# Divisors inverted per pair of token tiles, broadcasts in halves, and rotary sums on VectorE, in an attention block on one core

## Chip, cores and metric

The kernel runs on one core of a Trainium2 chip. The metric is the device time of one execution in microseconds, as the median of several runs.

## What is computed

For four batches of 1024 tokens and 512 channels, the reference does an attention block with a quantised linear layer behind it, each with a residual and a layernorm:

```python
q, k, v = X @ Wq, X @ Wk, X @ Wv               # 16 query heads, 8 key/value heads, 64 wide
q = q * cos + rotate_half(q) * sin             # the same for k
att = 50 * tanh((q @ k.T) / 16 / 50)           # causal mask, then softmax
y = (softmax(att) @ v).reshape(tokens, 1024) @ Wo
x = layernorm(X + y)
q8, scale = int8 of x per token (absmax / 127)
f = float16((q8 @ W8.T) * scale * w_scale + bias)
out = layernorm(x + f)
```

## The kernel before

All matrix products of the attention are done with operands split in a high and a low part of type fp32r (three products for one), written hi and lo in the names. The engines run programs of their own, each in the order written, and meet at semaphores. SyncE (SP) issues the loads and stores from its queue; ScalarE issues some from its own.

**Attention.** A batch is worked through in four units of four query heads and two key/value heads. A unit has 2 x 9 score tiles of 128 keys by up to 1024 query columns (both query heads of a group side by side), numbered s = 0 to 17 in the unit and g = 0 to 71 in the batch. The nine tiles of a key/value head cover four pairs of token tiles, c = 0 to 3 (256 queries each). For each tile TensorE makes the scores (L649), ScalarE takes tanh (L831) and exp (L836), GpSimd sets the causal mask on diagonal tiles (L1241), VectorE rounds to the high part (L1031) and subtracts to get the low part (L1035), and TensorE multiplies with v (L675) three tiles later (LAG). The row sums of the softmax come from a column of ones beside v. When a pair c of a head is finished, ScalarE copies sums and divisors (`keep_sums`, L850) and SP stores them in DRAM (`put_sums`: y_scratch in L447, d_scratch in L450).

**Rotary chunks.** While a unit runs, q and k of the next unit m are projected in three chunks x = 0 (k), 1 and 2 (q), 24 matmuls each, spread over tiles 0 to 2, 5 to 7 and 9 to 11 (L594). VectorE multiplies by cosine and sine (`rope_read`, at s = 3, 8, 12), GpSimd adds or subtracts the two products (`rotate`, L1218, L1221, L1223, at s = 4, 9, 13), ScalarE rounds (`round_rope`, L818, at s = 5, 10, 14), VectorE makes the low part (`rope_low`), and SP copies high and low part into place (`put`, eight DMAs each, L426 and L435). A buffer `work` has two places that alternate between the chunks. The chunks of the second unit of each later batch (m = 5, 9, 13) can't be put during the first unit of the batch in this way; they are projected at the end of the output stage before (`between(m)`), with the puts of x = 0 and 1 there and the rest in tiles 0 to 3.

**Passage.** After the last tile of a batch, TensorE projects v of the next batch (L620, tiles 0 to 4 before the first output tile, 5 to 7 after it; in the last batch there is none). SP loads the divisors of all token tiles (L538), VectorE inverts them (L1045), SP stores them (L546). For each of eight token tiles t, ScalarE's queue loads the reciprocals broadcast over 64 partitions, two DMAs of 256 KB (`load_rb`, L861) into the one buffer rb, SP loads y (L383, three buffers in `work`), GpSimd scales (L1254), ScalarE rounds (L871), VectorE makes the low part (L1049).

**Output stage.** Per token tile t: the product with Wo in two halves (L697), residual and layernorm statistics on VectorE (`residual1`, from L1057), 1/std on GpSimd (L1261, L1263), normalisation on ScalarE, quantisation on VectorE, transposition on TensorE (L707), `keep_q` on ScalarE (L891), the int8 linear layer (`linear`, L717) between the two halves of output tile t + 2, then rescaling, bias, residual and second layernorm. Wo's high and low part (2 MB each) are loaded over the q and k buffers from DRAM (L528, L532); after the first output tile SP loads w_scale, bias and the next unit's weights (w_ring).

The order of ScalarE's program around the stage:

```python
                load_rb(b, 0)
                load_rb(b, 1)
                round_y(b, 0)
                load_rb(b, 2)
                round_y(b, 1)
...
                    if t + 2 < NT:
                        load_rb(b, t + 2)
                    if t + 1 < NT:
                        round_y(b, t + 1)
...
                        keep_q(b, t - 2)
```

## Time and profile before

| | us |
|---|---|
| median of 3 runs (lowest, highest) | 1679.62 (1673.33, 1680.08) |
| profiled execution, its own time | 1678.03 |
| its span, first to last instruction | 1676.3 |
| busy: TensorE, VectorE, ScalarE, GpSimd | 1347.2, 1078.7, 838.9, 522.9 |

A row of the page's groups reads: line, engine and operation, output <- input, shapes, count | busy us in total, mean ns of one | idle time of the engine just before them <- what ended most of it. A row of the timeline reads: start us, duration us, engine, line, operation, output <- input, shapes, count, and in square brackets the idle time before it and its releaser. SPq and ACTq are the DMA queues of SyncE and ScalarE. PEclk is TensorE's granted clock as a share of 2.4 GHz. A row of the windows reads: stretch, its length, busy us (instructions) of PE, PEld, DVE, ACT and POOL, PEclk, busy share of the DMA engines, GB/s.

### The profile page before, as it was taken

To read this page: it belongs to the slowest core of one execution; us is meant where nothing else is said; L and a number is where in the kernel's file an instruction comes from. 1 tells how busy PE (TensorE), PEld (TensorE's weight loads), DVE (VectorE), ACT (ScalarE), POOL (GpSimd) and SP (SyncE) were. 2 spreads that over 40 slices of the span, in tenths; PEclk is the share of its full clock that TensorE was granted. 3 is DMA by queue.
4 is the path that set the end of the run, shared out by engine and by line. 5 is a ranking of instruction groups with operands and counts; after the bars stand their busy time and mean duration, and the time that the engine had idled before them with its cause. 6 is when DMAs were issued, how large, how long until landed. Compare 5 with 4: busy or idle time off the path is not lost.

```text
span 1676.3 us, 17436 instructions
## 1 busy us (share of the span) xinstructions
PE 1347.2 (80%) x5776; PEld 973.7 (58%) x5776; DVE 1078.7 (64%) x1242; ACT 838.9 (50%) x952; POOL 522.9 (31%) x525
## 2 busy tenths in 40 slices
PE   6389997966697999795768999898668799997565
PEld 5366674745464767564546676565445576764343
DVE  3287886843466888782455878776245688886244
ACT  4067666631127776562223867665122486786122
POOL 2351322212453133231245322212134413230244
PEclk9799998997798999898878999999787899999686
DMA  7764444375315244455423333636452514424331
GB/s 279 223 204 127 124 97 138 84 262 139 107 47 145 61 117 102 120 172 181 156 88 104 85 82 104 172 71 204 141 157 63 146 40 114 112 71 170 106 107 44
DMA packets 116138, 212.22 MB, mean 127 GB/s; under 512 B 22608, under 2 KB 65616, under 8 KB 111824
## 3 DMA queue, kind: packets, MB, share of 16 engines
q1 hardware_dynamic: 106320, 185.94, 38.6%
q10 hardware_dynamic: 9728, 25.17, 5.2%
q8 instruction: 46, 0.75, 0.2%
q14 instruction: 44, 0.36, 0.1%
HBM read 105.64 MB, written 38.27 MB: 86 GB/s over the span
## 4 chain that ended last, share of the span: by engine, by line
PE 54%; issue 10%; POOL 9%; DVE 8%; SPq 8%; DMA 5%; ACT 5%; ACTq 1%; POOLq 0%; DVEq 0%
PE ps L675 17%; PE ps L594 11%; PE ps L649 11%; PE ps L697 7%; PE ps L620 5%; SPq L435 4%; POOL y_raw L1254 3%; SPq L426 3%; PE ps L717 2%; ACTq L861 1%; ACT probs L831 1%; DMA x_raw<-X_T 1%; ACT probs L836 1%; POOL work L1223 1%; DMA d_scratch<-sums 1%
## 5 line engine op out<-in xcount | busy, mean ns | idle before, releaser
L675 PE MATMUL ps<-prob_hi,v 128*65 128x512 f32 (+3 forms) x1280 | 419.6, 377 | 31.4 <-DVE prob_lo L1035 31.2
L649 PE MATMUL ps<-qk 128*128 128x512 f32 (+1 forms) x1280 | 328.8, 385 | 80.8 <-ACT probs L831 52.6
L1035 DVE TENSOR_TENSOR prob_lo<-probs,prob_hi 128x1024 fp32r<-128x1024 f32 x288 | 382.8, 1329 | 9.9
L1241 POOL TENSOR_SCALAR_AFFINE_SELECT probs<-probs 128x256 f32<-128x256 f32 (+1 forms) x192 | 146.2, 769 | 699.0 <-ACT probs L836 699.0
L1031 DVE CAST prob_hi<-probs 128x1024 fp32r<-128x1024 f32 x288 | 261.0, 906 | 146.1 <-POOL probs L1241 96.9
L831 ACT ACTIVATE probs<-ps 128x1024 f32<-128x1024 f32 x288 | 292.1, 1014 | 78.2 <-PE ps L649 76.8
L649 PEld LDWEIGHTS ps<-qk 128*128 128x128 f32 x1280 | 230.4, 195 | 152.9 <-ACT probs L831 51.6
L836 ACT ACTIVATE probs<-probs 128x1024 f32<-128x1024 f32 x288 | 305.6, 1061 | 8.8
L594 PE MATMUL ps<-xT,w_ring 128*128 128x512 f32 x1152 | 293.5, 401 | 16.1 <-DVE xT L981 11.8
L697 PE MATMUL ps<-wo,y_hi 128*128 128x512 f32 x512 | 200.3, 475 | 72.2 <-issue 72.2
L594 PEld LDWEIGHTS ps<-xT,w_ring 128*128 128x128 f32 x1152 | 219.2, 193 | 64.5 <-DVE xT L981 12.5
L675 PEld LDWEIGHTS ps<-prob_hi,v 128*65 128x65 f32 (+1 forms) x1280 | 174.7, 138 | 134.3 <-DVE prob_lo L1035 49.1
L675 PE MATMUL ps<-prob_lo,v 128*65 128x512 f32 (+1 forms) x640 | 240.4, 376 | 0.0
L697 PEld LDWEIGHTS ps<-wo,y_hi 128*128 128x128 f32 x512 | 117.2, 233 | 105.7 <-issue 79.3
L818 ACT ACTIVATE work_r<-work 128x1024 fp32r<-128x1024 f32 x48 | 50.9, 1061 | 247.1 <-POOL work L1223 175.1
L871 ACT ACTIVATE y_hi<-y_raw 128x1024 fp32r<-128x1024 f32 x32 | 33.8, 1057 | 252.2 <-issue 222.4
L1049 DVE TENSOR_TENSOR y_lo<-y_raw,y_hi 128x1024 fp32r<-128x1024 f32 x32 | 39.2, 1225 | 172.5 <-ACT y_hi L871 172.5
L717 PE MATMUL ps<-ffn_wT,q16T 128*128 128x512 bf16 x128 | 51.4, 546 | 93.3 <-ACT q16T L891 93.3
L697 PE MATMUL ps<-wo,y_lo 128*128 128x512 f32 x256 | 117.3, 458 | 0.0
L675 PEld LDWEIGHTS ps<-prob_lo,v 128*65 128x65 f32 x640 | 88.6, 139 | 48.3 <-issue 1.8
L1254 POOL TENSOR_TENSOR y_raw<-y_raw,rb 128x1024 f32<-128x1024 f32 x32 | 75.4, 2356 | 121.0 <-DMA rb<-r_scratch 121.0
L620 PE MATMUL ps<-w_v,xT 128*128 128x512 f32 x384 | 91.5, 395 | 15.2 <-DVE w_v L1118 11.9
(69 smaller groups left out, 1097.2 us busy)
## 6 DMA issues: line engine op xcount, KB each, us to landing
qk<-work_r SPq DMA_DIRECT2D x256, 128.0 KB, 2.3
qk<-work_r SPq DMA_DIRECT2D x512, 64.0 KB, 2.0
y_scratch<-sums SPq DMA_DIRECT2D x256, 64.0 KB
wo<-wo_scratch SPq DMA_DIRECT2D x8, 2048.0 KB, 7.7
y_raw<-y_scratch SPq DMA_DIRECT2D x32, 512.0 KB, 3.6
rb<-r_scratch ACTq DMA_DIRECT2D x64, 256.0 KB, 4.0
w_ring<-w_scratch SPq DMA_DIRECT2D x15, 1024.0 KB, 5.2
x_raw<-X_T SPq DMA_DIRECT2D x16, 512.0 KB, 7.2
```

The source lines that it names most:

```text
L594: mm = nc.tensor.matmul(ps[:, bank + n, :], w_ring[:, slot, w, k, :], xT[:, a, k, half * HT:(half + 1) * HT], start=(k == w == a == 0), st ...
L620: mm = nc.tensor.matmul(ps[:, v_bank(t), :], xT[:, a, k, t * P:(t + 1) * P], weights[:, w, k, :], start=(k == a == w == 0), stop=(k == KC ...
L649: mm = nc.tensor.matmul(scores[:, g % 2, col:col + REP * w].rearrange("p (h q) -> p h q", h=REP), qk[:, n % 2, i, 2 + part, keys], qk[:, n ...
L675: mm = nc.tensor.matmul(sums_ps[:, :, GQ - w:GQ], v[:, kt, v0:v0 + width], p[:, g % ring, col:col + REP * w].rearrange("p (h q) -> p h q", ...
L697: mm = nc.tensor.matmul(bank, (y_lo[:, t % YRING, k, :] if a else y_hi[t % 2][:, k, :]), wo[:, w, k, :], start=(n == 0), stop=(n == 3 * KO ...
L717: mm = nc.tensor.matmul(ffn_ps, q16T[:, k, :], ffn_wT[:, k, :], start=(k == 0), stop=(k == KC - 1))
L831: nc.scalar.activation(probs[:, g % PRING, :], scores[:, g % 2, :], ACT.Tanh, scale=SCORE_SCALE / SOFTCAP).then_inc(capped, 1)
L836: nc.scalar.activation(probs[:, g % PRING, :], probs[:, g % PRING, :], ACT.Exp, scale=SOFTCAP).then_inc(exped, 1)
L1031: nc.vector.tensor_copy(prob_hi[:, g % HRING, :], probs[:, g % PRING, :]).then_inc(rounded, 1)
L1035: nc.vector.tensor_tensor(prob_lo[:, g % PRING, :], probs[:, g % PRING, :], prob_hi[:, g % HRING, :].bitcast(F32), ALU.subtract).then_inc( ...
L1241: nc.gpsimd.affine_select(out=diag, in_=diag, compare_op=ALU.is_ge, fill=0.0, base=0, pattern=[[0, n], [1, P]], channel_multiplier=-1).the ...
L1254: nc.gpsimd.tensor_tensor(y_raw[:, t % YRING, :, :], y_raw[:, t % YRING, :, :], rb[:, :, :], ALU.mult).then_inc(y_scaled, 1)
```

## The change

The divisors are loaded, inverted and stored per pair c of token tiles: pair 0 and 1 from within the last unit's tiles (SP at s = 15 and 17, VectorE at s = 17 and behind the last tile), pairs 2 and 3 in the passage. The reciprocals are broadcast by SP in halves of four heads' rows, into a ring of three half buffers; GpSimd scales in two halves. y tiles 0 and 1 are loaded in the last unit. v tiles 2 to 7 are projected two by two ahead of output tiles 0, 1 and 2. The rotary sums are done by VectorE within rope_read. Chunk x = 2 of the chunks between batches is projected in tiles 9 to 11 of the next batch's first unit like the others, and the puts of x = 0 and 1 stand in tiles 1 to 4 of that unit. The GpSimd path for low parts (POOL_LOW, never taken) is removed. The diff, cut:

```diff
+    RBRING = 3
-        rb = over("rb", "work", [P, KO, P], F32)
+        rb = [sb("rb0", [P, KO // 2, P]), over("rb1", "work", [P, KO // 2, P], F32),
+              over("rb2", "work", [P, KO // 2, P], F32, skip=2 * KB)]
-        div = sb("div", [P, P])
+        div = sb("div", [P, G, P // G])
+        def y_place(t):
+            return (t + 1) % YRING
-        def between(m):
-            return m == 0 or (m % UB == 1 and m > 1)
+        def between(m, x):
+            return m == 0 or (m % UB == 1 and m > 1 and x < 2)
...
+            def load_div(b, c):
+                n = groups_upto(b, NKV - 1, c)
+                sp.wait_ge(sums_put[0], 48 * ((n + 1) // 2))
+                sp.wait_ge(sums_put[1], 48 * (n // 2))
+                sp.dma_start(div[:, c, :], d_scratch[2 * c:2 * c + 2].rearrange("t h j (a n) -> (t h j a) n", n=P // G)
+                             ).then_inc(div_loaded[c], 16)
+
+            def store_div(b, c):
+                sp.wait_ge(div_done, divs_upto(b, c))
+                sp.dma_start(r_scratch[2 * c:2 * c + 2].rearrange("t h j (a n) -> (t h j a) n", n=P // G),
+                             div[:, c, :]).then_inc(div_stored[c], 16)
+
+            def load_rb(b, i):
+                t, e = divmod(i, 2)
+                if e == 0:
+                    sp.wait_ge(div_stored[t // 2], 16 * (b + 1))
+                if i >= RBRING:
+                    sp.wait_ge(y_scaled, halves_upto(b, 0, i - RBRING))
+                for h in range(REP):
+                    sp.dma_start(rb[i % RBRING][h * HD:(h + 1) * HD, :, :].rearrange("p k n -> p (k n)"),
+                                 r_scratch[t, h, e * KO // 2:(e + 1) * KO // 2].rearrange("k n -> (k n)")
+                                 .partition_broadcast(HD)).then_inc(rb_loaded[i % RBRING], 16)
...
+                        if b >= 1 and u == 0 and s in (1, 2, 3, 4):
+                            put(m, *((0, 0), (1, 0), (0, 1), (1, 1))[s - 1])
...
+                        if u == UB - 1 and s == 15:
+                            load_div(b, 0)
+                            wait_put(sp, last, 1)
+                            if b + 1 == B:
+                                wait_put(sp, last, 2)
+                            load_y(b, 0)
+                            load_y(b, 1)
+                        if u == UB - 1 and s == 17:
+                            load_div(b, 1)
+                            store_div(b, 0)
+
+                put_sums(b, NKV - 1, G - 2)
+                for x in range(3):
+                    wait_put(sp, last, x)
+                for i in range(RBRING):
+                    load_rb(b, i)
                 sp.wait_ge(scored, scores_upto(b, NB - 1))
                 sp.dma_start(wo[:, 1, :, :].rearrange("p k n -> p (k n)").bitcast(F32),
                              wo_scratch[:, KO * C:2 * KO * C]).then_inc(wo_lo_loaded, 16)
+                load_y(b, 2)
+                store_div(b, 1)
+                load_div(b, 2)
                 put_sums(b, NKV - 1, G - 1)
+                load_rb(b, 3)
+                load_div(b, 3)
                 for t in range(XRING):
                     load_x(b, t)
+                store_div(b, 2)
+                store_div(b, 3)
                 for t in range(NT):
-                    if t == 1 and b + 1 < B:
+                    if t == 2 and b + 1 < B:
...
+                    for i in (2 * t + 4, 2 * t + 5):
+                        if i < 2 * NT:
+                            load_rb(b, i)
                     if t + YRING < NT:
                         load_y(b, t + YRING)
                     if t + XRING < NT:
                         load_x(b, t + XRING)
...
@@ tensor @@
-                if more:
-                    for t in (2, 3, 4):
-                        project_v(b + 1, t)
                 for t in range(NT):
-                    if t == 1 and more:
-                        for n in (5, 6, 7):
-                            project_v(b + 1, n)
+                    if t <= 2 and more:
+                        project_v(b + 1, 2 * t + 2)
+                        project_v(b + 1, 2 * t + 3)
...
@@ scalar @@
-            def load_rb(b, t):
...
+                round_y(b, 0)
                 if more:
-                    for t in range(5):
-                        round_v(b + 1, t)
-                load_rb(b, 0)
-                load_rb(b, 1)
-                round_y(b, 0)
-                load_rb(b, 2)
+                    round_v(b + 1, 0)
+                    round_v(b + 1, 1)
                 round_y(b, 1)
...
@@ vector @@
                     nc.vector.tensor_tensor(crossed[HD:P], halves[0:HD], sin_k[HD:P], ALU.mult).then_inc(proj_read, 1)
+                    dve.wait_ge(proj_read, chunks_upto(m, x))
+                    nc.vector.tensor_tensor(turned, turned, crossed, ALU.add).then_inc(rotated, 1)
...
+                    dve.wait_ge(proj_read, chunks_upto(m, x))
+                    nc.vector.tensor_tensor(turned[:, 0, :], turned[:, 0, :], crossed[:, 0, :], ALU.subtract)
+                    nc.vector.tensor_tensor(turned[:, 1, :], turned[:, 1, :], crossed[:, 1, :],
+                                            ALU.add).then_inc(rotated, 1)
...
+            def invert(b, c):
+                dve.wait_ge(div_loaded[c], 16 * (b + 1))
+                nc.vector.reciprocal(div[:, c, :], div[:, c, :]).then_inc(div_done, 1)
...
+                        if u == UB - 1 and s == 17:
+                            invert(b, 0)
                         if g >= 1:
                             probs_of(b, g - 1)
...
                 probs_of(b, NB - 1)
+                invert(b, 1)
+                split_y(b, 0)
                 if more:
-                    for t in range(3):
-                        split_v(b + 1, t)
-                invert(b)
+                    split_v(b + 1, 0)
+                    split_v(b + 1, 1)
+                split_y(b, 1)
+                invert(b, 2)
                 if more:
-                    for t in (3, 4):
-                        split_v(b + 1, t)
-                split_y(b, 0)
-                split_y(b, 1)
+                    split_v(b + 1, 2)
+                    split_v(b + 1, 3)
                 residual1(b, 0)
+                invert(b, 3)
...
@@ gpsimd @@
-            def rotate(m, x):
...
             def scale_y(b, t):
                 pool.wait_ge(y_loaded[t % YRING], ring_upto(b, t, YRING))
-                pool.wait_ge(rb_loaded, 32 * rows_upto(b, t))
-                nc.gpsimd.tensor_tensor(y_raw[:, t % YRING, :, :], y_raw[:, t % YRING, :, :], rb[:, :, :],
-                                        ALU.mult).then_inc(y_scaled, 1)
+                for e in range(2):
+                    slot = (2 * t + e) % RBRING
+                    part = y_raw[:, y_place(t), e * KO // 2:(e + 1) * KO // 2, :]
+                    pool.wait_ge(rb_loaded[slot], rb_upto(b, t, e))
+                    nc.gpsimd.tensor_tensor(part, part, rb[slot][:, :, :], ALU.mult).then_inc(y_scaled, 1)
```

## Rows read from the trace of the kernel before

**Rows 1.** The page, busy time and share of the span.

```profile
PE 1347.2 (80%) x5776; PEld 973.7 (58%) x5776; DVE 1078.7 (64%) x1242; ACT 838.9 (50%) x952; POOL 522.9 (31%) x525
```

**Rows 2.** The page, groups of instructions by line.

```profile
L649 PE MATMUL ps<-qk 128*128 128x512 f32 (+1 forms) x1280 | 328.8, 385 | 80.8 <-ACT probs L831 52.6
...
L818 ACT ACTIVATE work_r<-work 128x1024 fp32r<-128x1024 f32 x48 | 50.9, 1061 | 247.1 <-POOL work L1223 175.1
```

**Rows 3.** Windows of batch 1's units and batch 0's passage (columns: see above).

```profile
560.00:620.00 60.00, 57.13 (x264) 41.35 (x264) 48.73 (x43) 40.47 (x44) 16.29 (x15) 1.00 0.41 104
350.00:385.00 35.00, 18.22 (x79) 13.79 (x79) 8.28 (x10) 5.88 (x9) 2.75 (x2) 0.79 0.61 187
```

**Rows 4.** Timeline of the passage of batch 0.

```profile
349.01 0.69 DVE L1031 CAST prob_hi<-probs 128x1024 fp32r<-128x1024 f32 x1
...
350.72 5.01 SPq L435 DMA_DIRECT2D qk<-work_r  x8
...
359.50 8.32 PE L620 MATMUL ps<-w_v,xT 128*128 128x512 f32 x36
...
366.12 0.95 DVE L1045 RECIPROCAL div<-div 128x128 f32<-128x128 f32 x1 [2.38 <-DMA div<-d_scratch]
...
373.67 8.41 ACTq L861 DMA_DIRECT2D rb<-r_scratch  x4
...
384.60 0.76 PE L697 MATMUL ps<-wo,y_hi 128*128 128x512 f32 x1 [16.78 <-issue]
```

**Rows 5.** DMA issues of the execution: KB each, median us to landing.

```profile
wo<-wo_scratch SPq DMA_DIRECT2D x8, 2048.0 KB, 7.7
...
rb<-r_scratch ACTq DMA_DIRECT2D x64, 256.0 KB, 4.0
...
div<-d_scratch SPq DMA_DIRECT2D x4, 64.0 KB, 1.7
r_scratch<-div SPq DMA_DIRECT2D x4, 64.0 KB, 6.0
```

**Rows 6.** Chain of waits, output stage of batch 0: one cycle of the loop.

```profile
422.16 0.70 DVE probs L1057
...
424.81 2.33 POOL y_raw L1254
...
427.15 0.45 ACTq L861
...
427.63 0.62 ACTq L861
...
431.84 4.35 PE ps L697 x12
```

**Rows 7.** Timeline: residual of output tile 2 in the last batch.

```profile
1594.59 0.69 DVE L1057 TENSOR_TENSOR probs<-ps,x_in 128x512 f32<-128x512 f32 x1 [1.76 <-PE ps L697]
```

**Rows 8.** Timeline of batch 0: the linear layer after a wait and without one.

```profile
470.45 1.89 PE L717 MATMUL ps<-ffn_wT,q16T 128*128 128x512 bf16 x4 [3.58 <-ACT q16T L891]
...
479.78 1.04 PE L717 MATMUL ps<-ffn_wT,q16T 128*128 128x512 bf16 x4
```

**Rows 9.** Timeline from batch 0 to batch 1.

```profile
496.57 5.84 PE L594 MATMUL ps<-xT,w_ring 128*128 128x512 f32 x24
...
508.24 1.02 ACT L831 ACTIVATE probs<-ps 128x1024 f32<-128x1024 f32 x1 [0.42 <-ACT probs L882]
...
513.96 1.23 DVE L1015 TENSOR_TENSOR work<-ps,cosT 128x1024 f32<-128x1024 f32 x1 [5.65 <-DMA qk<-work_r]
...
521.24 1.00 ACT L831 ACTIVATE probs<-ps 128x1024 f32<-128x1024 f32 x1
```

**Rows 10.** Timeline of a rotary chunk in batch 1's last unit.

```profile
729.27 1.78 DVE L1031 CAST prob_hi<-probs 128x1024 fp32r<-128x1024 f32 x1 [0.89 <-POOL probs L1241]
...
731.09 2.20 DVE L1035 TENSOR_TENSOR prob_lo<-probs,prob_hi 128x1024 fp32r<-128x1024 f32 x1
732.24 1.06 ACT L818 ACTIVATE work_r<-work 128x1024 fp32r<-128x1024 f32 x1 [5.10 <-POOL work L1223]
```

More of the change, by code:

```diff
@@ L87, in attention_block @@
     MASKS = [len(diagonals(s)) for s in range(NS)]
-    POOL_LOW = [False for s in range(NS)]
     LAG = 3
@@ L345, in ffn_tile, with chunk_at @@
             return ffn[:, -t % FRING, :]
-        def chunk_unit(b, u):
+        def chunk_at(b, u, s, steps):
             m = UB * b + u + 1
-            return m if m < U and not between(m) else None
+            if s in steps and m < U and not between(m, steps.index(s)):
+                return m, steps.index(s)
+            return None
         def group_in(b, g):
@@ L771, in _ @@
                 linear(b, NT - 1)
-                if more:
-                    project(m, 2, 0, 24)
         @block.scalar
@@ L956, in _ @@
                         norm2(b, t - 3)
-                m = UB * b + UB + 1
+                    if t == 1 and more:
+                        round_v(b + 1, 6)
+                        round_v(b + 1, 7)
                 store(b, NT - 4)
@@ L1189, in _ @@
                     residual1(b, t)
+                    if t == 1 and more:
+                        split_v(b + 1, 6)
+                        split_v(b + 1, 7)
                 m = UB * b + UB + 1
```

202 lines of the change are left out of this document (61 added, 141 removed).

## The prediction

> **What bounds the kernel now.** I read the page first. TensorE is busy 80% of the span and no other engine more than 64% [rows 1]: the reader is to look for the places where TensorE is the one that waits. The span is 1676.3 us, the profiled execution's own time 1678.03 us, and the median of the runs shown 1679.62 us, 1.6 us more; all sums below are made against 1678.
>
> The groups by line say who makes TensorE wait: 80.8 us ahead of the score matmuls, 52.6 of them for ScalarE's tanh; ScalarE in turn stood still 247 us ahead of its 48 rotary roundings (L818), 175 of them for GpSimd's sum at L1223 [rows 2]. Then the windows: in a unit of batch 1 TensorE is busy 57.1 of 60 us at the full clock, but where batch 0's attention gives way to its output projection it is busy 18.2 of 35 us, at a clock of 0.79 [rows 3]. Last the timelines and the chain of waits of three places: the passage into the output stage, the output loop, and the first tiles of the next batch.
>
> **The passage, before.** The timeline of batch 0 [rows 4]: the last copies of the rotated queries leave SP's queue at 355.7; the divisors of all tiles are inverted at 366.1, and the first broadcast starts only at 373.7, when their store has landed; scaling, rounding and the low part follow, and the first output matmul is at 384.6, after 16.8 us in which TensorE had nothing. The store took some 6 us to land although its mirror image, the load, took 1.7 [rows 5]: the store was issued behind three y tiles (512 KB each) and two x tiles (256 KB), 2 MB, on the same queue. The divisors had to wait for the sums of the last tile pair, which need the last score tile.
>
> **The passage, after.** Pair 0's sums are complete once head 7 has passed its second row block, so its divisors can be loaded as soon as SP is through with the copies. I leave their end at 355.7. The load is issued at 356.1 and lands at 357.9 (1.7 us); y tiles 0 and 1 go out by 357.0; a quarter of the reciprocal (0.95 us for all) is 0.3 us. VectorE stands at this inversion from 349.0 on, where the second last CAST now starts [rows 4], with the last two probability tiles (0.69 + 1.23 us each) behind it, and behind these TensorE's last two weighings: they end near 363.5, and not at 359.3 where the v projection now follows them. That costs nothing so long as the first y tile is later, and it is. The store goes out at 358.6 behind 1 MB instead of 2 MB; I take 4 us between its two bounds (1.7 and 6.0) and land it at 362.7. Three halves go out in six DMAs of 0.55 us each (0.45 and 0.62 [rows 6]); the first tile's two halves are in at 367.7, since a whole tile's pair takes 4.0 us [rows 5]. Two half scalings of 1.2 us each, the first one hidden, rounding 1.06, low part 1.23, then the low part of v tile 0, which the bank still waits for (0.7, as the 128x512 addition of [rows 7]): first output matmul at 372.1, 12.5 us earlier, with one v tile (a third of 8.32 us [rows 4]) fewer done before it.
>
> The later steps of this passage matter more. Tile 1's second half is issued behind the 2 MB of Wo's low half (7.7 us to land [rows 5]) and lands near 377, low part at 380.8. VectorE then inverts pair 2, splits v tiles 2 and 3, does the residual of tile 0 (384.1) and inverts pair 3; only then may SP, which stands in order at the store of pair 3, issue the broadcasts of tile 2. They land at 390, scaling ends 391.1, low part 393.4, quantising tile 0 ends 395.6, the residual of tile 1 at 397.3, GpSimd's rstd 398.3, and from there the loop's own chain (scale 2.4, round 1.06, keep q 0.6, linear 1.89 [rows 8], second half 4.35, hand-overs) gives the end of output tile 2 at 408.5. TensorE has done output tile 1 and v tiles 4 to 7 by 394.2, so it isn't the later one. Before, the same point was 422.2 [rows 6]: 13.7 us earlier, with all v work done in both. If the copies end earlier (they waited for the rotary too) this grows by up to 4, if the store takes its 6 us it shrinks by 2. I take 14, three times: **42 us**. In the last batch SP is free before the last tiles, nothing waits for v, and the same steps give the end of tile 2 at about 1582.5 against 1594.6 [rows 7]: **12 us**.
>
> **The output loop.** Its cycle in the chain of waits [rows 6]: output tile done (422.16), residual and statistics, GpSimd's scaling 2.33, ScalarE's queue issuing two broadcast DMAs 0.45 + 0.62, the rest of round_y and keep_q, linear, second half 4.35, next tile done at 436.2. The change takes the DMA issues off ScalarE's queue: 1.2 us with the hand-over. Splitting the scaling adds one small instruction start, 0.05. SP has the time, its queue is nearly empty there, and each half's slot is free one tile ahead. That holds for tiles 3, 4 and 5 (tile 2 is counted above; for 6 and 7 no broadcast stood in the way): 3 x 1.15 x 4 batches = **14 us**.
>
> **From one batch to the next.** Before [rows 9]: tile 0 of batch 1 gets its tanh at 508.2, tile 2 only at 521.2. VectorE stood in rope_read of the third chunk (513.96, 5.65 us for the first chunk's copies to leave the buffer) with the probabilities behind it, and ScalarE stood for GpSimd's sum of that chunk. After, this chunk is moved to tiles 9 to 14 of the unit. ScalarE then has tanh and exp of tile 0 (507.1 to 509.2), rounding, tile 1, rounding: tanh of tile 2 at 513.5, 7.7 us earlier. Given back: the chunk's 24 matmuls, 5.84 us, were free in the idle time and now stand in a TensorE-bound stretch. Net 1.6 us; the two ends are +5 (the chunk fills idle time) and -3 (the four copies, 5.0 us of SP each [rows 4], hold the sums back). Three times 1.3: **4 us**.
>
> **Rotary sums.** Taken from GpSimd (2.33 us for such a shape [rows 6]), given to VectorE as one TENSOR_TENSOR of 1.23 us or two of half the size: 48 x 1.3 = 62 us more on an engine that is busy 48.7 of 60 us in a unit [rows 3]. But a CAST beside a running sum took 1.78 us instead of 0.69 and the subtraction after it 2.20 instead of 1.23 [rows 4, 10], 2.06 us per chunk that VectorE gets back, so it comes out no busier. And ScalarE no longer waits 5.1 us per chunk of q [rows 10]. What TensorE gets of that is bounded by its own idle time: 52.6 us for tanh [rows 2], of which some is at the batch starts (counted) and some in waits that ScalarE has for other things. From 3 us idle of 60 in a unit [rows 3] I take 0.5 us for each of 12 units with a projection and one more for the first, between 0 and 25. **7 us.** In the prologue one sum stands alone in the chain: **1 us**.
>
> The Trainium skill (GPSIMD Engine Reference, Key points) says that GpSimd shares its SBUF interfaces with VectorE, with contention for two-port modes and for two SBUF inputs. By this rule the subtraction too is relieved, as the row of 2.20 us shows; taken alone, without relief, the added 62 us on VectorE would leave the term at 0 and the sum at 1605.
>
> **Sum.** 42 + 12 + 14 + 4 + 7 + 1 = 80; 1678 - 80 = 1598 us for the execution, 1599 for the median: faster by 4.8%.
>
> **Rivals.** (a) The broadcasts now share SP's queue with the bulk loads. For: a 64 KB store took 6.0 us behind 2 MB where the load took 1.7 [rows 5], and 2 MB of w_ring, w_scale and bias now go ahead of tile 4's broadcasts. Against: by my timetable these are 3.5 us early. If it is late by 4 us, and the first rows by 4 too, in three batches: 24 us lost, 1622. The Trainium skill (DMA: Bandwidth & Descriptors, Queues, rings and completion order) has SP and ScalarE own one ring row each, with packets taken in turn between rows, and ring order within one. By that rule a broadcast on SP can't pass a bulk load any more; the 6.0 us of the store agree with the order within a row, and no row here shows a broadcast passing.
> (b) The wait at the first inversion is longer, or VectorE falls behind in the tiles with a rotary: the head of its queue is now held 4 to 5 us (3.7 + 1.2) before a probability tile that TensorE needs two tiles later. If each of 45 chunks costs TensorE 1 us: 1598 + 45 = 1643. Against: each of the three tiles that carry a projection gives TensorE 8 matmuls, 1.9 us, beside its scores and weighings, so VectorE has time to catch up.
> (c) The other side: the same with 2.5 us per chunk, 112 us lost, 1710. It decides from 1.8 us per chunk on (80/45). Only if GpSimd's masks go on slowing VectorE as its sums did.
> (d) TensorE's clock: linear took 1.89 us at the low level and 1.04 at the full one [rows 8]; if the shorter waits of the loop leave the clock up for half of the tiles, 24 us more are won, 1574. Against: a wait of 3.58 us before linear was still followed by the low level.
> (e) The change doesn't bring the first rows forward, as SP comes late to load_div in any case: the passage is worth 6 instead of 14, total 1622.
>
> **Chances.** The forecast 0.60, alone 1582 to 1614 (the store and the copies' end +-6, the units -7 to +8, the batch starts +-3). (a) 0.12, (b) 0.08, (c) 0.03, (d) 0.10, (e) 0.07. The range 1572 to 1630 leaves out (b), (c) and the ends of (a) and (d), 0.17. A change under 0.5% (8 us) can't be told from none by this kernel's runs; slower by more is (c), 0.03, and 0.02 lies within it. Faster: 0.95.
>
> **What would show it.** Right: no DMA issue on ScalarE for rb; TensorE's wait before the first output matmul 2 to 6 us instead of 16.8; output tiles 12.7 us apart instead of 13.9; L818 with no wait for an engine over 2 us; no CAST of 1.78 us behind a rotary; tanh of tile 2 of a batch 6 us after tile 0, not 13. Wrong: VectorE as releaser of the weighings in the units; rb DMAs landing in more than 8 us; output tiles still 14 us apart, which would mean another hand-over ends last in the cycle.

## The result: faster by 7.0%, more than forecast

| | us |
|---|---|
| before, median of 4 runs | 1679.85 |
| after, median of 4 runs (lowest, highest) | 1561.72 (1557.29, 1562.36) |
| ratio, 95% interval | 0.930 (0.927 to 0.933) |
| profiled executions, before and after | 1678.03 and 1562.01 |

The forecast was 1599 (1572 to 1630): the direction is right, the gain is 116 us between the profiled executions and not 80. One execution of a later experiment (1643.82 us) had a granted clock of 0.80 throughout and is counted nowhere. The page of the changed kernel first, the lines that answer to [rows 1, 2] (the last one from the full list of groups):

```profile
PE 1317.1 (84%) x5776; PEld 965.0 (62%) x5776; DVE 1055.1 (68%) x1334; ACT 843.2 (54%) x952; POOL 378.6 (24%) x477
...
L688 PE MATMUL ps<-qk 128*128 128x512 f32 (+1 forms) x1280 | 328.2, 384 | 79.1 <-ACT probs L863 38.9
L863 ACT ACTIVATE probs<-ps 128x1024 f32<-128x1024 f32 x288 | 293.2, 1018 | 169.1 <-PE ps L688 167.7
L1052 DVE TENSOR_TENSOR prob_lo<-probs,prob_hi 128x1024 fp32r<-128x1024 f32 x288 | 356.6, 1238 | 9.9
...
L1048 DVE CAST prob_hi<-probs 128x1024 fp32r<-128x1024 f32 x288 | 203.3, 706 | 136.5 <-POOL probs L1246 79.7
...
L850 ACT ACTIVATE work_r<-work 128x1024 fp32r<-128x1024 f32 x48 | 50.1, 1044 | 33.9 <-DVE work L1022 17.7 <-DVE work L1032 16.2
```

ScalarE's rounding of the rotary sums (L818 before, L850 now) stood still for 247 us and now for 34, and GpSimd is no longer among its releasers; all of the 34 lie in the prologue. VectorE does 48 more sums and yet is busy 24 us less: the CAST takes 706 ns in the mean and the subtraction 1238. Before, it was 906 and 1329, and 40 of the 288 CASTs took more than 1.7 us, against one after:

```profile
L1035 DVE TENSOR_TENSOR prob_lo<-probs,prob_hi 128x1024 fp32r<-128x1024 f32 x288 | 382.8, 1329 | 9.9
...
L1031 DVE CAST prob_hi<-probs 128x1024 fp32r<-128x1024 f32 x288 | 261.0, 906 | 146.1 <-POOL probs L1241 96.9
```

In ScalarE's row for tanh (L863) the engine waits for TensorE's scores, 168 us: in the units it is TensorE that sets the pace.

**Where the 116 us are.** The table gives distances in us between landmarks that both timelines have: ScalarE's tanh of a unit's first tile, of tile 71, and the residual of an output tile.

| | before | after | gain | forecast |
|---|---|---|---|---|
| tile 71 to residual of tile 2, batches 0, 1, 2 | 73.3, 72.0, 72.0 | 58.8, 60.4, 58.7 | 39.5 | 42 |
| the same, batch 3 | 61.3 | 48.8 | 12.5 | 12 |
| residual of tile 2 to that of tile 6, four batches | 217.3 | 195.4 | 21.9 | 14 |
| last residual to next batch, three | 23.4 each | 21.8 each | 4.6 | 4 |
| sixteen units, first tile to first (or to tile 71) | 974.6 | 937.6 | 37.0 | 7 |
| prologue | 83.5 | 83.0 | 0.5 | 1 |

The rows add up to 116.0. Of the 36 us that the forecast lacks, the units carry 30 and the loop 8; the other terms are within 3. The units' 37.0 us are no even share: the second units of the batches gain 5 us each, units 2 and 3 mostly 2 to 4, and the first units nothing. Windows over one unit, the second of batch 3, from tanh to tanh, first before and then after (columns as in [rows 3]):

```profile
1369.10:1432.40 63.30, 60.42 (x279) 43.73 (x278) 51.18 (x46) 43.12 (x48) 17.20 (x18) 1.00 0.40 101
```

```profile
1279.10:1337.10 58.00, 58.00 (x274) 43.17 (x273) 49.48 (x52) 43.64 (x49) 9.80 (x13) 1.00 0.46 117
```

From tanh to tanh it is 63.3 and 58.0 us, both at the full clock. After, TensorE has no idle time at all; before, the window shows 2.9 us of it (63.30 - 60.42) and 5.3 were won. The two windows don't hold quite the same matmuls, though (279 and 274): the next unit's first tanh comes 2.57 us after its scores have begun before the change and 1.77 after it. TensorE's own distance, from the unit's first score matmul to the next unit's (1367.73 to 1429.83 and 1277.37 to 1335.33, 272 matmuls each), is 62.10 and 57.96 us. So TensorE won 4.1 us here, still 1.3 more than the 2.9 that are drawn as idle, in four waits. Part of the reason is in the timeline of the kernel before, start and duration ahead of the engine's name:

```profile
1391.63 0.39 PE L675 MATMUL ps<-prob_hi,v 128*65 128x512 f32 x1
1391.86 0.40 PE L675 MATMUL ps<-prob_lo,v 128*65 128x512 f32 x1
```

A matmul is drawn 0.39 us long though the next one starts 0.23 after it, so its drawn end covers the first 0.16 us of every wait behind it: 0.64 us for the four waits drawn, and shorter waits aren't drawn at all (six starts in the unit are 0.28 to 0.34 us behind the one before, with no idle time drawn). Over the twelve units with a full projection (a batch's last unit measured to its last score matmul) the distances fell from 786.0 to 750.3 us, 35.7, and the drawn idle time from 66.2 to 44.8, only 21.4.

**The passage** in the timeline of batch 0, to be laid beside [rows 4]:

```profile
343.79 1.86 SPq L467 DMA_DIRECT2D qk<-work_r  x3
345.75 0.53 SPq L398 DMA_DIRECT2D div<-d_scratch  x1
...
347.80 0.35 DVE L1061 RECIPROCAL div<-div 128x32 f32<-128x32 f32 x1 [8.09 <-DMA div<-d_scratch]
348.18 0.32 SPq L403 DMA_DIRECT2D r_scratch<-div  x1
351.50 3.71 SPq L413 DMA_DIRECT2D rb<-r_scratch  x6
...
355.06 1.29 POOL L1256 TENSOR_TENSOR y_raw<-y_raw,rb 128x512 f32<-128x512 f32 x1 [12.77 <-DMA rb<-r_scratch]
...
361.03 0.47 PE L736 MATMUL ps<-wo,y_hi 128*128 128x512 f32 x1 [2.12 <-DVE v L997]
```

The order forecast holds step by step, all of it 9.3 us earlier because batch 0's units were shorter: the divisors' load, forecast at 356.1 less 9.3, starts at 345.75; the store leads to the first broadcast in 3.3 us (4 were taken); the first output matmul, at 372.1 less 9.3 = 362.8 by the forecast, is at 361.03, behind a wait of 2.12 us instead of 16.78, and the last thing it waits for is the low part of v, as said. VectorE stood 8.09 us at the first inversion. Windows of the same 35 us as in [rows 3]: TensorE is busy 32.3 of them instead of 18.2, at a clock of 0.95 instead of 0.79 (of the 35 us that start 9.3 us earlier, at the same point of the work, 32.2 at 0.89).

```profile
350.00:385.00 35.00, 32.30 (x133) 25.06 (x132) 11.79 (x19) 8.27 (x13) 8.42 (x8) 0.95 0.61 190
```

**The loop**, one cycle of the chain of waits, as in [rows 6]:

```profile
398.39 0.70 DVE probs L1073
...
401.04 2.46 POOL y_raw L1256 x2
403.52 0.03 ACT y_hi L890
...
404.49 0.59 ACT q16T L910
...
405.12 1.04 PE ps L756 x4
406.16 4.35 PE ps L736 x12
```

ScalarE's two DMA issues (0.45 and 0.62) are gone, the two half scalings cost 2.46 instead of 2.33, and the linear layer takes 1.04 us in this cycle, where before it took 1.89 in nearly every one ([rows 8], the first). The broadcasts land in 3.3 us at the median:

```profile
rb<-r_scratch SPq DMA_DIRECT2D x128, 128.0 KB, 3.3
```

The median hides the ones behind the next unit's weights on SP's queue: in the three batches with a next one, tile 4's four broadcasts follow the weights and take 7.8 to 9.7 us, ten of the twelve over 8. GpSimd waits for them only once, 0.77 us, here in the chain of waits and the timeline of batch 1:

```profile
767.58 9.74 DMA rb<-r_scratch
```

```profile
777.45 2.48 POOL L1256 TENSOR_TENSOR y_raw<-y_raw,rb 128x512 f32<-128x512 f32 x2 [0.77 <-DMA rb<-r_scratch]
```

### The profile page after: what moved, and what is told of

The parts are those of the page before. It is cut to its first block, busy times and chain, and to the rows that moved or that the text cites. A ratio compares the mean times of both kernels' runs of the same rounds, so it can differ in the third digit from the quotient of the medians.

```text
span 1560.3 us, 17566 instructions
## 1 busy us (share of the span) xinstructions
PE 1317.1 (84%) x5776; PEld 965.0 (62%) x5776; DVE 1055.1 (68%) x1334; ACT 843.2 (54%) x952; POOL 378.6 (24%) x477
## 4 chain that ended last, share of the span: by engine, by line
PE 48%; SPq 13%; DVE 13%; POOL 8%; DMA 7%; issue 7%; ACT 4%; POOLq 0%; DVEq 0%; ACTq 0%
PE ps L714 18%; PE ps L633 12%; PE ps L688 12%; SPq L467 7%; POOL y_raw L1256 4%; DMA rb<-r_scratch 3%; PE ps L736 3%; SPq L480 2%; PE ps L659 2%; SPq L413 1%; DVE prob_hi L1048 1%; DVE work_r L1038 1%; PE ps L756 1%; POOL rstd L1264 1%; DMA x_raw<-X_T 1%
## 5 line engine op out<-in xcount | busy, mean ns | idle before, releaser
L863 ACT ACTIVATE probs<-ps 128x1024 f32<-128x1024 f32 x288 | 293.2, 1018 | 169.1 <-PE ps L688 167.7
L1052 DVE TENSOR_TENSOR prob_lo<-probs,prob_hi 128x1024 fp32r<-128x1024 f32 x288 | 356.6, 1238 | 9.9
L1048 DVE CAST prob_hi<-probs 128x1024 fp32r<-128x1024 f32 x288 | 203.3, 706 | 136.5 <-POOL probs L1246 79.7
L633 PEld LDWEIGHTS ps<-xT,w_ring 128*128 128x128 f32 x1152 | 218.7, 192 | 63.4 <-DVE xT L992 15.3
L736 PE MATMUL ps<-wo,y_hi 128*128 128x512 f32 x512 | 186.4, 446 | 14.9 <-issue 7.6
L890 ACT ACTIVATE y_hi<-y_raw 128x1024 fp32r<-128x1024 f32 x32 | 33.8, 1058 | 213.3 <-POOL y_raw L1256 213.3
L736 PEld LDWEIGHTS ps<-wo,y_hi 128*128 128x128 f32 x512 | 107.8, 215 | 45.0 <-issue 17.5
L882 ACT ACTIVATE sums<-ps 65x512 f32<-65x512 f32 x128 | 74.6, 583 | 94.7 <-PE ps L714 71.3
L756 PE MATMUL ps<-ffn_wT,q16T 128*128 128x512 bf16 x128 | 45.6, 494 | 78.7 <-ACT q16T L910 78.7
L659 PE MATMUL ps<-w_v,xT 128*128 128x512 f32 x384 | 96.3, 409 | 16.8 <-DVE w_v L1134 11.9
L736 PE MATMUL ps<-wo,y_lo 128*128 128x512 f32 x256 | 109.3, 427 | 0.0
L1256 POOL TENSOR_TENSOR y_raw<-y_raw,rb 128x512 f32<-128x512 f32 x64 | 80.4, 1272 | 96.8 <-DMA rb<-r_scratch 96.8
```

Of the source, the lines that this page charges most:

```text
L633: mm = nc.tensor.matmul(ps[:, bank + n, :], w_ring[:, slot, w, k, :], xT[:, a, k, half * HT:(half + 1) * HT], start=(k == w == a == 0), st ...
L659: mm = nc.tensor.matmul(ps[:, v_bank(t), :], xT[:, a, k, t * P:(t + 1) * P], weights[:, w, k, :], start=(k == a == w == 0), stop=(k == KC ...
L736: mm = nc.tensor.matmul(bank, (y_lo[:, y_place(t), k, :] if a else y_hi[t % 2][:, k, :]), wo[:, w, k, :], start=(n == 0), stop=(n == 3 * K ...
L863: nc.scalar.activation(probs[:, g % PRING, :], scores[:, g % 2, :], ACT.Tanh, scale=SCORE_SCALE / SOFTCAP).then_inc(capped, 1)
L1048: nc.vector.tensor_copy(prob_hi[:, g % HRING, :], probs[:, g % PRING, :]).then_inc(rounded, 1)
L1052: nc.vector.tensor_tensor(prob_lo[:, g % PRING, :], probs[:, g % PRING, :], prob_hi[:, g % HRING, :].bitcast(F32), ALU.subtract).then_inc( ...
```

## Experiments

The kernel before ran again beside each set of experiments, with medians of 1679.4, 1675.3 and 1680.2 us. The ratios below are to the one beside them; differences in us are between medians, so those across sets are good to some 5 us. Distances inside a kernel are those of its profiled execution.

### The sums alone, taken back and done alone

The first two kernels differ from the changed kernel and from the one before by who adds the rotary products:

```diff
-                    nc.vector.tensor_tensor(turned, turned, crossed, ALU.add).then_inc(rotated, 1)
...
+                        if at := chunk_at(b, u, s, (4, 9, 13)):
+                            rotate(*at)
```

```diff
+                    nc.vector.tensor_tensor(turned, turned, crossed, ALU.add).then_inc(rotated, 1)
...
-                        if m is not None and s in (4, 9, 13):
-                            rotate(m, (4, 9, 13).index(s))
```

> The changed kernel with the rotary sums back on GpSimd, at tiles 4, 9 and 13 as before; all else as changed. Theory: the units with a projection gained 36.7 us against the kernel before because of where the sums are done, by ScalarE's wait, by VectorE's slowing, or both. Then they return to 62 to 69 us each, the batch starts lose 2 or 3 us each too, and the time is 1562 + 37 + 8 = 1607 us, 1598 to 1616. Rival: the gain of the units came with the reordering of the queues (puts, the moved chunk), and only my 7 us hang on the sums: 1569 to 1575.

> The kernel before with the rotary sums on VectorE within rope_read and nothing else changed. Theory: the units gain the same 35 to 40 us as in the changed kernel, and the batch starts up to 4 us each: 1680 - 45 = 1635 us, 1627 to 1645. Rival (the prediction's own term): 8 us, 1672. Second rival: the sums help only together with the reordered puts, under 15 us: over 1665.

Measured: taken back 1611.33 us (ratio to before 0.960, 0.956 to 0.963), 50 us above the changed kernel; alone 1639.0 (0.976, 0.974 to 0.978), 40 us below the kernel before. The units are 45.9 us longer in the one and 37.7 shorter in the other. So the edit that the forecast priced at 7 + 1 us is worth 40 to 50. The groups of the run with the sums taken back:

```profile
L1046 DVE TENSOR_TENSOR prob_lo<-probs,prob_hi 128x1024 fp32r<-128x1024 f32 x288 | 383.1, 1330 | 9.9
...
L1042 DVE CAST prob_hi<-probs 128x1024 fp32r<-128x1024 f32 x288 | 261.7, 909 | 163.0 <-POOL probs L1253 112.7
...
L850 ACT ACTIVATE work_r<-work 128x1024 fp32r<-128x1024 f32 x48 | 50.8, 1058 | 202.7 <-POOL work L1235 143.5
```

Two things come back together: VectorE's CAST is longer (909 ns for 706), and ScalarE stands 202.7 us ahead of its roundings, all of it for GpSimd's sums. The next two runs part them.

### Sums on GpSimd that nobody waits for

```diff
+                        if at := chunk_at(b, u, s, (4, 9, 13)):
+                            pool.wait_ge(proj_read, chunks_upto(*at))
...
+                            for half in range(2):
...
+                                nc.gpsimd.tensor_tensor(rb[0][:, :, :].rearrange("p k n -> p (k n)"),
+                                                        cosT[:, cols], sinT[:, cols], ALU.add).then_inc(spared, 1)
```

The changed kernel, with 39 pairs of additions on GpSimd at the places where the rotary sums stood. They write into a free buffer, and nothing reads them.

> The changed kernel plus, at tiles 4, 9 and 13, two additions of 128x512 f32 on GpSimd that wait for the same event as the sums did, write a buffer that nobody reads, and that nobody waits for (39 times). GpSimd's masks after them can be late by up to 2.5 us. Theory A (ScalarE's wait made the loss): nothing waits here, 1562 to 1566 us. Theory B (GpSimd's sum slows VectorE's CAST and subtraction by 2 us and TensorE waits for that): 20 to 35 us of the 37 come back, 1582 to 1597, and CASTs of 1.7 us and more stand beside the additions.

Measured: 1582.24 us (0.942, 0.939 to 0.945), 20.5 above the changed kernel, as the second theory had it; the units are 21.7 longer.

```profile
L1054 DVE TENSOR_TENSOR prob_lo<-probs,prob_hi 128x1024 fp32r<-128x1024 f32 x288 | 398.3, 1383 | 9.9
...
L1050 DVE CAST prob_hi<-probs 128x1024 fp32r<-128x1024 f32 x288 | 249.9, 868 | 89.2 <-POOL probs L1248 55.9
...
L1322 POOL TENSOR_TENSOR rb<-cosT,sinT 128x512 f32<-128x512 f32 x78 | 136.3, 1748 | 3.1
```

The CAST takes 868 ns and the subtraction 1383 for 706 and 1238: 288 x (0.162 + 0.145) = 88 us of VectorE's time for 136 us of GpSimd's. A two-input operation of GpSimd beside VectorE costs time though nothing waits for it. There is one other way in which the additions could cost time: GpSimd's masks stand behind them. The timeline of the second unit of batch 3 shows what each does:

```profile
1345.29 2.20 DVE L1054 TENSOR_TENSOR prob_lo<-probs,prob_hi 128x1024 fp32r<-128x1024 f32 x1
...
1347.54 0.44 PE L716 MATMUL ps<-prob_hi,v 128*65 128x512 f32 x1 [1.05 <-DVE prob_lo L1054]
...
1348.02 0.69 DVE L1050 CAST prob_hi<-probs 128x1024 fp32r<-128x1024 f32 x1 [0.53 <-POOL probs L1248]
```

TensorE's longest wait of the unit, 1.05 us, ends with the stretched subtraction; the late mask then holds VectorE for 0.53 us, and in the whole execution VectorE stands less for masks than in the changed kernel (55.9 us for 79.7). So here it is the slowed VectorE. That some 21 us of the 46 in the units are of this kind is an estimate all the same: here VectorE did its own sums besides.

By the Trainium skill (GPSIMD Engine Reference, Key points) GpSimd shares its SBUF interfaces with VectorE, with contention for VectorE's instructions that have two SBUF inputs or run in a two-port mode. The trace agrees for the subtraction, which has two inputs. The CAST has one and was slowed as much; which mode it runs in no run here shows.

### Sums on GpSimd, with ScalarE asking later

The sums are on GpSimd as in the first experiment, and rounding, low parts and copies come one or two tiles later:

```diff
...
-                        if at := chunk_at(b, u, s, (5, 10, 14)):
+                        if at := chunk_at(b, u, s, (7, 12, 15)):
                             round_rope(*at)
...
-                        if at := chunk_at(b, u, s, (6, 11, 15)):
+                        if at := chunk_at(b, u, s, (8, 13, 16)):
                             rope_low(*at)
...
```

> The changed kernel with the rotary sums back on GpSimd (as in the run that gave 1611.3), and ScalarE's rounding of each sum and the steps behind it one or two key tiles later (tiles 7, 12, 15 for 5, 10, 14, the low parts a tile later), so that ScalarE does not reach the rounding before GpSimd's sum is done. It tells apart the two halves of the 46 us that units lost with the sums on GpSimd. Theory: some 21 us are VectorE's and GpSimd's contention (measured by idle sums nobody reads) and some 24 us ScalarE standing for the sum. Then ScalarE's idle time at the rounding behind GpSimd (143.5 us in that run) falls to below 50, and the time is 1590 to 1600. Rival: the sum's slowness costs by contention alone, and the standing is only where idle time shows: then about 1611, within 5 us.

Measured: 1623.33 us (0.966, 0.964 to 0.968). The total is a miss. ScalarE's wait fell as intended, to 53.0 us from 202.7, but another came: the copies now leave so late that the next unit's scores wait for them. In the timeline of batch 1 sixteen copies stand in SP's queue for 10 us at a change of unit, and TensorE waits 3.33 us:

```profile
604.68 10.13 SPq L467 DMA_DIRECT2D qk<-work_r  x16
...
613.77 1.46 PE L688 MATMUL ps<-qk 128*128 128x512 f32 x4 [3.33 <-DMA qk<-work_r]
```

The units, one by one, separate what the total mixes. Batch 1, us:

| | unit 0 | unit 1 | unit 2 | unit 3 | tile 71 to residual of tile 0 |
|---|---|---|---|---|---|
| changed kernel | 48.9 | 58.0 | 66.5 | 64.1 | 35.2 |
| unread sums on GpSimd | 49.0 | 59.9 | 68.2 | 65.9 | 33.2 |
| sums on GpSimd | 52.6 | 63.0 | 68.5 | 66.7 | 33.1 |
| the same, rounded later | 50.0 | 59.3 | 73.9 | 63.0 | 40.2 |

In units 0 and 1 rounding later gives back 6.3 of 8.7 us. What is left there, 2.4 us together, is near the 2.0 that the unread sums cost, though not unit by unit (1.1 and 1.3, against 0.1 and 1.9). In batches 2 and 3 it gives back 5.4 of 7.8 and 5.1 of 7.7, and leaves the same. Unit 2 and the passage lose 5.4 and 7.1 against the sums on GpSimd, to the late copies; unit 3 gains 3.7. So in units 0 and 1 the greater part of the loss goes when ScalarE no longer stands for the sum. The edit moves the low parts and the copies as well, and what their places are worth was not measured; for the other units the division is argued from these two.

### Who issues the broadcasts

```diff
+            def load_rb(b, i):
+                t = i // 2
+                act.wait_ge(div_stored[t // 2], 16 * (b + 1))
+                act.wait_ge(y_scaled, halves_upto(b, t - 1, 1))
...
+                    if t + 2 < NT:
+                        load_rb(b, 2 * t + 5)
                     if t + 1 < NT:
                         round_y(b, t + 1)
```

> The changed kernel with the second half's broadcast of tiles 3 to 7 (two DMAs, about 1.1 us) issued by ScalarE ahead of round_y and behind both scalings, where the kernel before had its broadcasts. Theory: this issue time was in the loop's cycle, and 8 of the 22 us that the loop gained are TensorE's clock, which the shorter wait leaves up more often: tiles 3 to 6 go from 12.1 to 13.4 us or more, 1562 + 14 to 22 = 1576 to 1584 us. If the issue alone counts and the clock has another cause: 1574 to 1578. Rival: halves have made the chain wait elsewhere, and the issue costs nothing: 1562.

> The changed kernel with the second half's broadcast of token tiles 3 to 7 issued by ScalarE ahead of its rounding of y; its time was 1590.5 to 1595.8, and its trace is wanted at the full granted clock. If the loss lies in the output loop, its tiles 3 to 6 take 13.2 to 13.6 us each against 11.4 to 13.0 of the changed kernel, with VectorE's scaling of the second half waiting for that broadcast; units and passages are as in the changed kernel.

Measured: 1590.53, 1591.89 and 1595.76 us (ratio 0.948, 0.946 to 0.951), in another set 1593.75 once. That is 30 us more than the changed kernel, where 14 to 22 were expected. (The second expectation has a slip: it is GpSimd that scales, not VectorE. Its 13.2 to 13.6 us per tile are a miss too: tiles 3 to 6 took 11.5 to 14.1.) ScalarE's instructions in one cycle:

```profile
435.87 1.10 ACTq L889 DMA_DIRECT2D rb<-r_scratch  x2
437.07 1.06 ACT L899 ACTIVATE y_hi<-y_raw 128x1024 fp32r<-128x1024 f32 x1 [6.63 <-issue]
...
438.04 0.58 ACT L919 ACTIVATE q16T<-ps 128x512 bf16<-128x512 bf16 x1
...
438.67 1.89 PE L756 MATMUL ps<-ffn_wT,q16T 128*128 128x512 bf16 x4 [4.96 <-ACT q16T L919]
```

GpSimd's scaling has ended when the issue starts, since its end is what frees the buffer; then come 1.10 us of issuing, and only then rounding, quantised tile and linear layer. From residual 0 to residual 6 the four batches take 326.8 us for 296.3. Of these 30.5 us, 6.7 lie in the linear layers and the second halves behind them, at TensorE's lower level; the other 24 are 1.2 us for each of the 20 issues, the forecast's own 1.2 per tile.

### The passage

In both kernels VectorE inverts pair 0 behind the last probability tile:

```diff
-                        if u == UB - 1 and s == 17:
-                            invert(b, 0)
...
                 probs_of(b, NB - 1)
+                invert(b, 0)
                 invert(b, 1)
```

In the second one SP's part goes back behind the last pair's sums as well, and the first broadcasts behind all of it:

```diff
-                        if u == UB - 1 and s == 15:
-                            load_div(b, 0)
...
-                            load_y(b, 0)
-                            load_y(b, 1)
...
                 put_sums(b, NKV - 1, G - 1)
+                for c in (3, 0, 1, 2):
+                    load_div(b, c)
...
+                for t in range(YRING):
+                    load_y(b, t)
```

> The changed kernel with VectorE's first inversion behind the last probability tile instead of ahead of the last two. In the changed kernel VectorE stood 8.1 us there in batch 0. Theory: that wait costs nothing, as pair 0's divisors land no earlier in either (347.8 in batch 0, when both tiles would be done) and the first y tile is what the output waits for: within 3 us of 1562 in batches 0 to 2, and in the last batch, where the divisors land sooner, up to 3 us lost: 1560 to 1566. Rival (b of the prediction): TensorE's late weighings hold the passage, so up to 5 us per batch are won: 1542 to 1555.

> The changed kernel with every load of divisors and of y behind the sums of the last pair, as before; broadcasts in halves from SP, v tiles and rotary sums stay as changed. Theory: the passage's gain (39.6 us in three batches and 12.5 in the last by the distances of the residuals) comes from the early pair: 40 to 48 us are lost, 1602 to 1610. Rival: halves, their ring and the order of v tiles carry half of it: 1580 to 1590.

Measured: with the inversion of pair 0 behind the last probability tile 1565.11 us (0.934, 0.931 to 0.936), an interval that overlaps that of the changed kernel, so that by the time alone nothing is shown; in the trace of batch 3, where no v stands behind it, tile 71 to the first residual is 28.5 us for 23.4.

With all loads of divisors and y behind the last pair's sums 1616.11 (0.964, 0.961 to 0.967), 54 above and more than the 40 to 48 expected. Its profiled execution, the shortest of six, took 1606.62, 44.6 above that of the changed kernel. Tile 71 to the first residual takes 43.4, 42.9, 43.8 and 36.9 us for 33.8, 35.2, 33.3 and 23.4, which is 41 of these. So the first residual's gain hangs on bringing the first rows forward: halves, v order and sums alone leave it where it was (before: 44.3, 43.3, 43.2, 37.9).

To the residual of tile 2, the landmark of the forecast, it is otherwise: 66.9, 66.8, 67.3 and 60.1 us, where the kernel before took 73.3, 72.0, 72.0 and 61.3. So 16.3 of the 39.5 us of three batches stay without the early pair. They come from the other edits of the stage, which no run separates. Part is paid back at tile 3, which takes 15.4, 15.0 and 15.8 us in these batches for 12.1, 13.0 and 11.5: the scaling of tile 4 stands in that cycle, and its broadcasts, issued behind the next unit's weights, take up to 9.95 us to land.

### Better than both

In the changed kernel SP stands at the stores of pairs 2 and 3 until VectorE has inverted these, with the broadcasts of token tile 2 behind them, although tile 2 belongs to pair 1, inverted long before. The edit lets them pass; the second version also takes the next unit's weights out of the way of tile 4's.

```diff
                 for t in range(XRING):
                     load_x(b, t)
+                load_rb(b, 4)
+                load_rb(b, 5)
                 store_div(b, 2)
                 store_div(b, 3)
...
-                        load_wk(UB * b + UB + 1)
-                        load_wq(UB * b + UB + 1)
                     for i in (2 * t + 4, 2 * t + 5):
-                        if i < 2 * NT:
+                        if 6 <= i < 2 * NT:
                             load_rb(b, i)
+                    if t == 2 and b + 1 < B:
+                        load_wk(UB * b + UB + 1)
+                        load_wq(UB * b + UB + 1)
```

> The changed kernel with the two broadcasts of tile 2 issued by SP ahead of the stores of pairs 2 and 3, at which SP stood until VectorE had inverted pair 3 (375.1 in batch 0). Theory (the prediction's timetable of the passage): scaling of tile 2 starts some 3.5 us earlier, bounded by GpSimd's first inverse_std, and residual 1 of tile 1 with it: 3.5 x 4 = 14 us won, 1548 us, 1544 to 1554. Rival: TensorE's v tiles or Wo's low half bound tile 1 and nothing moves: 1562.

> Both edits (inversion behind the last tile, broadcasts of tile 2 ahead of the stores). By the theories of the two alone 1546 to 1552 us. If TensorE's late weighings start to bound once the broadcasts are early, more than the sum: 1538 to 1545.

> The changed kernel with the broadcasts of pairs of token tiles issued ahead of the stores of the inverted divisors (as in the run that gave 1548.7) and the key and query weights of the next unit loaded behind the last broadcasts of the passage, not in front of tile 4's. In that run output tile 3 took 14.9 to 16.1 us against 12 for its neighbours, with a broadcast of tile 4 of 9.66 us behind weight loads. If the weight loads were what it stood behind, tile 3 takes 11 to 12.5 us in the three passages between batches, which is some 4 us by 3, and the time is 1534 to 1540. Rival: the broadcasts stand behind something else, or the weights come too late for the first projection of the next batch: 1548 or above, and the distance from the last residual to the next batch's first tile grows from 21.8 us.

Measured: the first two lines alone 1548.74 us (0.924, 0.922 to 0.927), 13 below the changed kernel by the medians, 9 by the ratios (0.930 less 0.924); with the late inversion as well 1557.2 (0.929, 0.926 to 0.931), a miss: where the broadcasts are early, the late inversion costs some 8 us; with the weights last 1544.69 (0.919, 0.917 to 0.922), the fastest kernel of this study, by 4 us between medians and 9 by the ratios. It was expected at 1534 to 1540. In the first version output tile 1 took 9.4 us instead of 13, but tile 3 took 14.9, 16.1 and 15.3 in the batches with a next one. Its chain of waits there:

```profile
383.05 0.43 SPq L423
...
383.53 0.43 SPq L428
...
384.06 1.08 SPq L413
...
385.19 9.66 DMA rb<-r_scratch
```

L423 and L428 are the loads of the next unit's key and query weights, L413 the two broadcasts of tile 4: issued right behind them on the same queue, these take 9.66 us to land, where the median is 3.3. This is rival (a) of the forecast. The changed kernel has the same slow broadcasts, but there they were early by more than they lost; with the tiles ahead shorter, TensorE waits for them. With the weights last tile 3 takes 13.2, 13.0 and 12.5 us, 7.7 us less together. 5.1 us of it go again to tiles 2 and 4, and tile 3 is now an ordinary cycle with the linear layer at 1.73 to 1.89 us, which is why the 11 to 12.5 expected were not reached. The weights were not late: the next batch still starts 21.8 us behind the last residual.

## Why the prediction was off

**The step that failed** is the paragraph on the rotary sums, in its last sentences: "What TensorE gets of that is bounded by its own idle time ... From 3 us idle of 60 in a unit I take 0.5 us for each of 12 units", 7 us between 0 and 25. The units gave 37.0, above even the upper bound. Both mechanisms that it names were right: the contention (21 us by the unread sums) and ScalarE's standing for the sum (the greater part in units 0 and 1). Three sizes were wrong. The idle time of 3 us per unit, read in one unit, is less than TensorE could gain, 4.1 in the unit above, in part because the drawn matmul ends hide the start of each wait. The bound of 25 counted only the 52.6 us ahead of the scores; the waits ahead of the weighings behind VectorE's low part, 31.2 us before and 8.3 after, were left out (before, then after):

```profile
L675 PE MATMUL ps<-prob_hi,v 128*65 128x512 f32 (+3 forms) x1280 | 419.6, 377 | 31.4 <-DVE prob_lo L1035 31.2
```

```profile
L714 PE MATMUL ps<-prob_hi,v 128*65 128x512 f32 (+3 forms) x1280 | 419.4, 377 | 8.3 <-DVE prob_lo L1052 8.3
```

And of the 3 us visible only 0.5 was taken, with no row behind that choice. This is the size that counts: all 3 us for each of the 12 units would have given 36 us.

**The passages**, 42 and 12, measured 39.5 and 12.5. The timetable was within 2 us at each step shown above, and that SP would hold the broadcasts of tile 2 until the store of pair 3 was in it too; the prediction did not ask whether this order was needed.

**The loop**, 14, measured 21.9. Over these four tiles of four batches the linear layers and the second halves behind them took 97.4 us before and 85.5 after, 11.9 less for the same instructions: that part is TensorE's clock, rival (d). The linear layer ran at the full level in 6 of the 16 cycles, and in none of them before. The remaining 10.0 are what the term of 14 meant. From residual to linear layer 9 of the 12 cycles counted take 6.73 us for 7.79, 1.06 less and not 1.15, because the split scaling costs 0.13 and not 0.05. The other three give 0.3 to 0.6: one waits for the broadcast of 9.74 us shown above, and in two GpSimd still works at the second layernorm of an earlier tile when the next one could start. The cycle of tile 6, counted at nothing, lost 1.0 us in the four batches. Rival (d) was priced at 24 with a chance of 0.10 and gave half of that.

**From one batch to the next**, 4: measured 1.5 each, 4.6. The tanh of tile 2 comes 5.9 us after that of tile 0 and not 13.0; unit 0 of batches 1 to 3 stays at 48.9, because the chunk's matmuls now stand in it. (7.7 less 5.84 is 1.9, not the 1.6 of the prediction; the term stays within its ends.)

**The rivals.** (a) did come about as a mechanism: ten broadcasts took more than 8 us, which the prediction names as a sign of being wrong. But they had the slack that it counted on, and the price was 0.8 us and not 24; in the first improved kernel it was more. (b) and (c) needed VectorE to fall behind. It waited 8.09 us at the first inversion, but moving that inversion behind the tiles won nothing (1565.11 us), and with the broadcasts early it lost some 8; in the units no such loss is seen, TensorE being busy 58.0 of 58.0 us in the one above. (e) was false: the first rows did come forward, 10.5 us at the first residual of batch 0. The condition under which VectorE's additional 62 us would leave the term at 0, no relief, did not come about: it is busy less, 1055.1 us for 1078.7.

## What to carry to other kernels

Idle time drawn before a matmul is a lower bound: compare the same work between two landmarks of TensorE with what its instructions need at their closest spacing (here 58.0 us of 62.1). Where the waits are those of the engines that a change relieves, expect all of it back and not a sixth; waits for something else stay, as the 44.8 us still drawn in the twelve units show. Elementwise work of GpSimd with two inputs had a price here even though nobody waited for it; try it on VectorE where that engine has a few us to spare in each unit. In a queue that several consumers share, put a store that waits for a late result behind every load that is already due, and bulk loads behind small urgent ones.

## What was not expected of the hardware

The clock level of the linear layer does not follow from the length of the wait before it. In batch 0 of the changed kernel a wait of 3.40 us is followed by the low level (granted clock 0.50) and one of 3.72 by the full one (1.00), and three cycles further, at 441.33, a wait of 3.72 by the low one again, while in the same batch before the change waits of 3.58 us ([rows 8]) and of 4.8 us were followed by the low one:

```profile
393.13 1.89 PE L756 MATMUL ps<-ffn_wT,q16T 128*128 128x512 bf16 x4 [3.40 <-ACT q16T L910]
...
405.12 1.04 PE L756 MATMUL ps<-ffn_wT,q16T 128*128 128x512 bf16 x4 [3.72 <-ACT q16T L910]
```

Nor does the full level there hold for the whole cycle. From the linear layer's end to the residual, which the second half sets, it is 3.37 us in the first of these cycles (395.02 to 398.39, granted clock 0.83) and 4.37 in the second (406.16 to 410.53, 0.61): the low stretch moves from the one to the other, and the two together take 5.26 and 5.41 us. In batch 0 before the change both were long in these cycles, 1.89 and 4.1 to 4.6. What decides this stays open; no run here was made for it.
